# First layer's weighted sums: adding up in PSUM instead of in SBUF

## The reference, cut to what matters

```python
ex = jnp.exp(scores - seg_max[dst])
denom = jax.ops.segment_sum(ex, dst, num_segments=N)
w = ex / denom[dst]
agg = jax.ops.segment_sum(w[:, :, None] * V[src], dst, num_segments=N)
deg = jax.ops.segment_sum(jnp.ones((src.shape[0],), jnp.float32), dst, num_segments=N)
msgs = jnp.where(deg[:, None, None] > 0, agg, V)
```

## Time and profile before

| what | us |
|---|---|
| median of 3 timed runs | 5717.69 (5707.19 to 5718.29) |
| profiled execution: its span, first to last instruction (the page gives no other time of it) | 5709.5 |
| TensorE busy, of the span | 4142.4 (73%) |
| VectorE busy | 2438.6 (43%) |
| GpSimd busy | 2168.6 (38%) |
| ScalarE busy | 1163.7 (20%) |
| `attend_phase`, first instruction to the next phase's first | 900.0 to 1266.8 |

### The profile page before, as it was taken

How to read it: one execution, slowest core, us unless ns; L and a number is a source line. 1 busy time by engine, 2 the same in 40 slices (tenths; PEclk the granted TensorE clock), 3 DMA queues, 4 the chain that set the end, 5 groups by cost and what they waited for, 6 DMA issues and landing times. The chain is left out here.

```text
span 5709.5 us, 67954 instructions
## 1 busy us (share of the span) xinstructions
PE 4142.4 (73%) x19769; PEld 3142.0 (55%) x19769; DVE 2438.6 (43%) x4746; ACT 1163.7 (20%) x2671; POOL 2168.6 (38%) x2090
## 2 busy tenths in 40 slices
PE   5788884654816666799976999455559999555668
PEld 2555553443614444599975888333437677334445
DVE  4577778877234444356655000421223222212244
ACT  1233330001220000232322444100004333000023
POOL 0566654554436666000000210466650000566621
PEclk9888887996958888899986999677779999777789
DMA  2677874530743223210012998233330000233310
GB/s 77 208 243 241 250 215 151 162 98 23 235 128 88 85 86 86 86 38 8 7 41 82 336 323 281 89 88 93 87 97 26 1 1 16 75 91 88 91 37 23
DMA packets 375879, 639.34 MB, mean 112 GB/s; under 512 B 73053, under 2 KB 270072, under 8 KB 375424
## 3 DMA queue, kind: packets, MB, share of 16 engines
q1 hardware_dynamic: 275262, 342.97, 18.4%
q0 software_dynamic: 100288, 292.14, 17.6%
HBM read 526.37 MB, written 108.57 MB: 111 GB/s over the span
## 5 line engine op out<-in xcount | busy, mean ns | idle before, releaser
L2554 PE MATMUL sum_ps<-gathered_rows,hit 128*125 (+1 forms) x3328 | 1061.5, 477 | 842.0 <-issue 561.2
L2468 POOL DMA_INDIRECT gathered_rows<-k_table,index x1176 | 1160.8, 987 | 1281.1 <-ACT index L2457 717.6
L2554 PEld LDWEIGHTS sum_ps<-gathered_rows,hit 128*125 128x125 f32 (+1 forms) x3328 | 744.9, 235 | 1158.0 <-issue 1033.1
L97 POOL DMA_INDIRECT rows_all<-kv_table,src_of_visit x416 | 448.5, 1078 | 310.6 <-issue 135.5
L2538 DVE TENSOR_TENSOR node_sums<-node_sums,sum_ps 125x256 f32 x244 | 102.3, 419 | 918.0 <-DMA composed<-in_L_gnn_b 495.7
L2457 ACT ACTIVATE index<-src_of_chunk 128x4 int32<-128x4 int32 x294 | 59.2, 205 | 1647.0 <-DMA gathered_rows<-k_table,index 1581.1
L777 PE MATMUL ps_q<-q,hit_t 125*128 x832 | 322.5, 473 | 5.9 <-issue 5.2
L1057 PE MATMUL ps_sum<-summand,hit 128*125 128x261 f32 x832 | 211.6, 397 | 147.1 <-DVE odd_sums L1017 123.2
L2538 DVE TENSOR_TENSOR window_sums<-window_sums,sum_ps 126x256 f32 x344 | 144.8, 421 | 348.2 <-PE sum_ps L2554 183.0
L2762 PE MATMUL qk_ps<-window_sums,composed 128*128 128x126 f32 (+1 forms) x2400 | 292.1, 279 | 0.0
L1996 DVE TENSOR_TENSOR y<-out_ps,b 128x256 f32<-128x256 f32 x120 | 50.9, 424 | 551.2 <-PE out_ps L1895 464.0
(11 more groups left out here) (478 smaller groups left out, 6714.6 us busy)
## 6 DMA issues: line engine op xcount, KB each, us to landing
w<-in_L_ffn_W SPq DMA_DIRECT2D x112, 1024.0 KB
v_kept<-rows_all SPq DMA_DIRECT2D x104, 512.0 KB
v_rows<-v_kept SPq DMA_DIRECT2D x104, 512.0 KB, 3.6
gathered_rows<-k_table,index POOLq DMA_INDIRECT x1176
w<-in_L_ffn_w SPq DMA_DIRECT2D x64, 256.0 KB
b<-in_L_ffn_b SPq DMA_DIRECT2D x88, 128.0 KB
y_slots<-y SPq DMA_DIRECT2D x32, 256.0 KB
y_slots<-y SPq DMA_DIRECT2D x56, 128.0 KB
```

The source lines that it names most:

```text
L97: pool.indirect_dma_start(env.ring[:, k % KEPT_RING, i, :], None, env.kv_table, bass.IndirectOffsetOnAxis(env.src_of_visit[:, k * VB + i:k ...
L2468: pool.indirect_dma_start(self.rows[:, (q % SLOTS) * CHUNKS + c, :], None, self.table, bass.IndirectOffsetOnAxis(self.index[:, q % SLOTS, ...
L2554: mm = pe.matmul(sum_ps[0:rows, k % banks, 0:D], hit[:, g % (lead + 1), i * chunks + c, :], gather.rows[:, ds(first[i] + c, 1), :].rearran ...
```

## The change

Eight PSUM banks (`SUM_BANKS`) replace the two batches of four. A visit's bank is its tile number modulo 8, and every matmul adds onto what the bank holds (`start=False`). VectorE clears all banks once at the start of the phase and no longer adds; it makes the hits and, in ScalarE's place, copies the weights into `summand`. TensorE loads, per batch, the four bank numbers in one call and the last visit's tile number plus one (`turn_of_visit`) in another, and waits until so many banks have been cleared. ScalarE goes through the 25 tiles: it loads the number of the tile's last visit (`end_of_tile`), waits until so many visits have been multiplied, copies the bank to `sums`, and writes zeros over the bank. `odd_sums` and its final add are gone. `setup_phase` computes the three new tables in five VectorE instructions and one transpose on TensorE.

```diff
+                    if out is None:
+                        done(v.tensor_copy(bank_i[:], tile_bc[j][0:1, :]))
+                        done(v.tensor_scalar(env.bank_of_visit[:], bank_i[:], SUM_BANKS - 1, None, ALU.bitwise_and))
+                        done(v.tensor_scalar(env.turn_of_visit[:], tile_bc[j][0:1, :], 1.0, None, ALU.add))
+                        done(v.memset(env.end_of_tile[:], VT))
+                        done(v.tensor_copy(env.end_of_tile[:, 0:T - 1], bank[1][0:1, 441:440 + T]))
...
+                    if j == 0:
+                        pe.transpose(bank[1][0:1, 440:440 + T], key[0:T, 0:1], env.ident[0:T, 0:T])
...
-        odd_sums = sb(env, st, "odd_sums", [P, T, VC])
-        sum_of = [env.sums, odd_sums]
-        ps_sum = ps(env, st, "ps_sum", [128, 2, VB, 512])
+        ps_sum = ps(env, st, "ps_sum", [128, SUM_BANKS, 512])
...
             def _(v):
-                def add(k, tiles):
...
-                        v.tensor_tensor(here, here, ps_sum[0:P, k % 2, i, 0:VC], ALU.add).then_inc(summed, 1)
...
-                v.memset(env.sums[:], 0.0).then_inc(cleared, 1)
-                v.memset(odd_sums[:], 0.0).then_inc(cleared, 1)
...
-                v.tensor_tensor(env.sums[:], env.sums[:], odd_sums[:], ALU.add)
+                v.memset(ps_sum[:], 0.0).then_inc(filled, 1)
+                v.wait_ge(filled, 2)
+                for k in range(batches):
+                    if k >= SLOTS:
+                        v.wait_ge(multiplied, (k - SLOTS + 1) * VB)
                     make_hits(v, env, hit[:, k % SLOTS], env.rel_dst, 128, k).then_inc(hits_made, 1)
+                    v.tensor_copy(summand[:, k % SLOTS, :, D:D + HEADS], env.scores[:, k * VB:(k + 1) * VB, :]).then_inc(copied, 1)
             def _(act):
+                act.wait_ge(filled, 2)
+                act.sem_inc(cleared, SUM_BANKS)
+                for t in range(T):
+                    here = ps_sum[0:P, t % SUM_BANKS, 0:VC]
+                    upto = act.value_load(env.end_of_tile[0:1, t:t + 1], min_val=1, max_val=VT)
+                    act.wait_ge(multiplied, upto)
+                    act.activation(env.sums[:, t, :], here, ACT.Copy).then_inc(kept, 1)
+                    if t + SUM_BANKS < T:
+                        act.wait_ge(kept, t + 1)
+                        act.activation(here, env.ones[0:P, 0:1].to_broadcast([P, VC]), ACT.Copy, scale=0.0).then_inc(cleared, 1)
             def _(pe):
+                pe.wait_ge(filled, 2)
                 for k in range(batches):
                     slot = k % SLOTS
+                    _, banks = nc.values_load_multi_w_load_instructions(env.bank_of_visit[0:1, k * VB:(k + 1) * VB],
+                                                                        engines=[mybir.EngineType.PE], min_val=0, max_val=SUM_BANKS - 1)
+                    turn = pe.value_load(env.turn_of_visit[0:1, k * VB + VB - 1:(k + 1) * VB], min_val=1, max_val=T)
+                    pe.wait_ge(cleared, turn)
                     pe.wait_ge(hits_made, k + 1)
+                    pe.wait_ge(copied, k + 1)
                     pe.wait_ge(weighed, k + 1)
-                    if k >= 2:
-                        pe.wait_ge(summed, (k - 1) * VB)
                     for i in range(VB):
-                        mm = pe.matmul(ps_sum[0:P, k % 2, i, 0:VC], hit[:, slot, i, 0:P], summand[:, slot, i, :],
-                                       start=True, stop=True)
-                    mm.then_inc(multiplied, 1)
+                        pe.matmul(ps_sum[0:P, ds(banks[i], 1), 0:VC].rearrange("p o n -> p (o n)"), hit[:, slot, i, 0:P],
+                                  summand[:, slot, i, :], start=False, stop=True, skip_group_check=True).then_inc(multiplied, 1)
```

More of the change, by code:

```diff
@@ L200, in setup_phase @@
         key = sb(env, st, "key", [128, 4])
+        bank_i = sb(env, st, "bank_i", [1, VT_PAD], I32)
         cmp = [sb(env, st, f"cmp{j}", [128, -(-c // 128), v]) for j, (_, _, c, v, _) in enumerate(passes)]
@@ L807, in _ @@
                 batch_loop(act, batches, SLOTS, one_batch)
+SUM_BANKS = 8
 RUNS = 32
@@ L969, in attend_phase @@
         summand = sb(env, st, "summand", [128, SLOTS, VB, VC])
-        odd_sums = sb(env, st, "odd_sums", [P, T, VC])
-        sum_of = [env.sums, odd_sums]
-        ps_sum = ps(env, st, "ps_sum", [128, 2, VB, 512])
-        cleared, hits_made, multiplied, summed, weighed, copied = [ph.sem() for _ in range(6)]
+        ps_sum = ps(env, st, "ps_sum", [128, SUM_BANKS, 512])
+        filled, hits_made, multiplied, weighed, copied, cleared, kept = [ph.sem() for _ in range(7)]
         own_landed = ph.sem()
@@ L992, in _ @@
             def _(pool):
-                pool.memset(summand[:], 1.0).then_inc(cleared, 1)
-                pool.wait_ge(cleared, 3)
+                pool.memset(summand[:], 1.0).then_inc(filled, 1)
+                pool.wait_ge(filled, 2)
                 for k in range(batches):
@@ L998, in _ @@
                     if k >= SLOTS:
-                        pool.wait_ge(multiplied, k - SLOTS + 1)
+                        pool.wait_ge(multiplied, (k - SLOTS + 1) * VB)
                     pool.tensor_tensor(summand[:, slot, :, 0:D].rearrange("p v (h d) -> p v h d", h=HEADS),
@@ L1006, in _ @@
             def _(v):
-                def tile_of(k, i):
-                    return v.value_load(env.tile_of_visit[0:1, k * VB + i:k * VB + i + 1], min_val=0, max_val=T - 1)
-                def add(k, tiles):
[L1012 to L1016, removed]
-                        v.tensor_tensor(here, here, ps_sum[0:P, k % 2, i, 0:VC], ALU.add).then_inc(summed, 1)
-                        if k + 1 < batches:
-                            following.append(tile_of(k + 1, i))
-                    return following
@@ L1022, in hits @@
-                def hits(k):
-                    make_hits(v, env, hit[:, k % SLOTS], env.rel_dst, 128, k).then_inc(hits_made, 1)
-                v.memset(env.sums[:], 0.0).then_inc(cleared, 1)
-                v.memset(odd_sums[:], 0.0).then_inc(cleared, 1)
[L1027 to L1035, removed]
@@ L1036, in _ @@
-                v.wait_ge(summed, batches * VB)
-                v.tensor_tensor(env.sums[:], env.sums[:], odd_sums[:], ALU.add)
+                v.memset(ps_sum[:], 0.0).then_inc(filled, 1)
[3 more added lines that the diff above has]
+                        v.wait_ge(multiplied, (k - SLOTS + 1) * VB)
+                    make_hits(v, env, hit[:, k % SLOTS], env.rel_dst, 128, k).then_inc(hits_made, 1)
+                    v.tensor_copy(summand[:, k % SLOTS, :, D:D + HEADS], env.scores[:, k * VB:(k + 1) * VB, :]).then_inc(copied, 1)
@@ L1051, in _ @@
                     pe.wait_ge(hits_made, k + 1)
+                    pe.wait_ge(copied, k + 1)
                     pe.wait_ge(weighed, k + 1)
-                    pe.wait_ge(copied, k + 1)
-                    if k >= 2:
-                        pe.wait_ge(summed, (k - 1) * VB)
                     for i in range(VB):
-                        mm = pe.matmul(ps_sum[0:P, k % 2, i, 0:VC], hit[:, slot, i, 0:P], summand[:, slot, i, :],
-                                       start=True, stop=True)
@@ L3339, in build @@
         env.tile_of_visit = sb(env, x_stack, "tile_of_visit", [1, VT_PAD], I32)
+        env.bank_of_visit = sb(env, x_stack, "bank_of_visit", [1, VT_PAD], I32)
+        env.turn_of_visit = sb(env, x_stack, "turn_of_visit", [1, VT_PAD], I32)
+        env.end_of_tile = sb(env, x_stack, "end_of_tile", [1, T], I32)
         env.src_of_visit = sb(env, x_stack, "src_of_visit", [128, VT_PAD], I32)
```

## The result

The changed kernel takes 5659.26 us (median of 4 runs, 5657.38 to 5668.87); the kernel before, on the same chip, 5717.99 us (4 runs, 5707.19 to 5721.81). The ratio is 0.9909, with a 95% interval of 0.9893 to 0.9924: faster by 0.9%, and 3 us from the forecast of 5662. The profiled execution took 5658.99 us with a span of 5657.1, against a span of 5709.5 before. Of the four executions of four_loads, further down, one took 11185.87 us; its ratio leaves that one out, its median does not.

The account below looks back on a forecast made before the run. VectorE's hits and adds bound the kernel before; TensorE's instruction queue would bound it next. Loop -39.7, head -8.5, tail -9.0 and setup +1.7 gave -55.5 us, from the median 5717.7 to 5662 us; range 5600 to 5700.

Parts of the forecast that it names:

- the loop: The 104 batches of the changed phase: time per batch p falls from 3.285 to 2.9 us, -39.7 us.
- the head: Phase start to first passes: one shorter memset, first passes at 907.8 instead of 916.33 us, -8.5 us.
- the tail: Last pass to next phase: only the last copy, 1.1 us instead of 10.1, -9.0 us.
- setup: Setup phase: five added VectorE instructions, which TensorE waits for, lie on the path, +1.7 us (0 to 2.5).
- ScalarE's banks: Loop: waiting for ScalarE to copy and zero a bank costs nothing; 17 us in all if ScalarE were not ahead.
- GpSimd: Loop: GpSimd's products take 1.9 us each, with about 1 us idle, waiting for TensorE.
- The pair's rule: Loop: GpSimd and VectorE take turns, so p is at least 2.3 us, 2.5 if the scores copy waits too.
- Rival 1: Loop: checks cost little, GpSimd and VectorE bound it; p 2.4, 5611 us, up to 5640; chance 0.20.
- Rival 2: Loop: the call becomes four loads, TensorE's queue is slower than VectorE was; p 3.9, 5765 us; chance 0.11.
- Rival 3: Loop: register loads are slower than 0.3 us; p 3.2 to 3.3, 5693 to 5703 us; chance 0.07.

Follow-up runs that it names:

- four_loads: The changed kernel with four loads of one bank number each in place of one load of four: ratio 1.0111 to the kernel before.
- three_bank_checks: The changed kernel with one of the four bank-number range checks left out: batch time 2.700 us at the mean, 2.647 at the median.
- no_bank_checks: The changed kernel with the four bank numbers loaded without range checks, the tile number's check kept: median batch time 2.385 us.
- hits_from_psum: no_checks_reduce with the hit reading iota from PSUM and four sum banks instead of eight: batch time 1.859 us at the median, 2.108 at the mean.
- no_checks_reduce: The changed kernel with bank numbers unchecked and VectorE's copy of scores made by a reduction: median batch time 2.307 us.

## Why the prediction was right

The mechanism of the loop, the head and the tail held; the loop was off by 6.9 us and setup, whose step failed, by 2.1 the other way. The four terms of the sum came to -51.6 us instead of -55.5. That the median lies only 3 us from the forecast is in part luck: the gain by the spans is 52.4 us, by the medians 58.7, and the score phase alone scatters by 21.

- **The loop.** Forecast p 2.9 and -39.7 us, measured 2.967 and -32.8. TensorE's queue is what the forecast named, with one load and four checks as it was read from the way the call is written. The term is mis-sized by 0.067 us a batch, 6.9 us in all, and most of that is rounding: the forecast's own parts, 2.0 for a group of two loads, 0.84 for three checks and 0.10 for one more wait, add up to 2.94, the median measured is 2.951, and it took 2.9. A check costs 0.28 as forecast (0.27 to 0.30 by three_bank_checks); a load of four registers is 0.04 longer than one of one. The mean lies 0.016 above the median, 1.6 us in the loop: the first batch took 3.63 us, and some others 3.05 to 3.11, whose cause stays open.
- **ScalarE's banks,** costed at nothing, cost nothing that the trace shows: the four waits that bear its name are gaps of the usual 0.9 to 1.0 us.
- **GpSimd.** The prediction looked for products of 1.9 us with about 1 us idle. They took 2.35 with 0.6 idle, since each still meets a hit. With the queue as the bound this did not touch the time.
- **The head.** Forecast -8.5, measured -9.0. First passes were forecast 7.8 us behind the phase's start and came at 7.3. The memset of PSUM took 3.47 us for 4096 columns; 3.45 was worked out from the SBUF memset of the earlier trace rows. The estimate of 4.26 us, worked out from the 1.04 ns that the Trainium skill (PSUM — Partial Sum Buffer, "Specifications (TRN2)") gives for a 2-byte element, is not what this memset of 4-byte elements shows; the measurement decides.
- **The tail.** Forecast -9.0, measured -9.4: the copy of 0.39 us, and 0.3 us from its end to the next phase.
- **Setup.** The step that failed: +1.7 us was forecast "on the path", -0.4 measured. The five instructions cost what was said and did delay TensorE, but what they delay is not what ends the phase. Setup in after, then in before:

```profile
28.47 0.43 SPq L231 DMA_DIRECT2D x<-in_x  x1
...
51.67 0.50 PEld L374 LDWEIGHTS bank<-sel,rows_f 98*128 98x128 f32 x2 [4.42 <-DVE sel L310]
...
66.12 4.98 SPq L233 DMA_DIRECT2D quad_key_kept<-quad_key  x1
...
78.06 1.08 DVE L1265 BATCH_NORM_STATS2 moments_nodes<-x 125x6 f32<-125x256 f32 x3 [2.36 <-DVEq L501]
```

```profile
28.25 0.43 SPq L230 DMA_DIRECT2D x<-in_x  x1
...
64.01 7.44 SPq L232 DMA_DIRECT2D quad_key_kept<-quad_key  x1
...
78.40 0.75 DVE L1272 BATCH_NORM_STATS2 moments_nodes<-x 125x6 f32<-125x256 f32 x2 [4.83 <-DVEq L492]
```

The weight load of `sel` came 1.8 us later (51.67, 49.88 in the earlier trace rows). VectorE had 4.83 us to spare before the next phase and has 2.36 left. SyncE waits there for two transfers, the load of `x`, issued long before the five instructions (28.25 and 28.47 us), and the store of `quad_key`, which stands behind it in the same queue. The trace's packets show which is late. The last of the 3125 rows of `x` (1,024 bytes each) landed at 76.70 us before and 76.36 after, the last eight of the store's 128 packets came behind them, until 77.34 and 76.99, and the next phase began 0.93 to 0.94 us later. That distance, and the 1.57 to 1.58 us from the last row of `x`, are the same in all eleven profiled executions. So the end of `x` sets the phase's end, and the store, issued 2.1 us later, still finds itself waiting behind it. In the ten executions with the five instructions the next phase began at 77.6 to 79.4 us, in the one without at 78.3: the -0.4 is scatter, and the cost is hidden. That the forecast asked only whether TensorE waits, and not what the barrier waits for, was the mistake.
- **The pair's rule.** The Trainium skill (SBUF — State Buffer, "Who interferes with whom") says that a VectorE instruction of the kinds named in the prediction and a GpSimd instruction that reads SBUF exclude each other. The trace agrees: the copy takes 1.87 us beside a product and 0.16 without one, and with one hit input in PSUM hit and product fall to 0.69 and 1.91 us; whether the copy runs in a two-port mode no run shows. The pair did not set the time of after; with the copy in it its floor is 2.385 us, as no_bank_checks shows, below the 2.5 that the prediction drew from the rule.
- **The rivals.** Rival 1 (p 2.4) did not come, since the checks are paid; its bound shows in the kernel without bank checks, 2.468 at the mean. Rival 2 is four_loads. Rival 3, slow loads, did not come: after's loads keep 0.30 to 0.35 us.

## What to carry to other kernels

A loop whose instructions take register values can be bound by an engine's instruction queue, which no busy share shows: add up loads, checks and waits of one turn, and compare the sum with the turn. Ask for neighbouring words in one load, and leave the range check out where the making of the value already bounds it (here the low three bits of a tile number): that gave 0.57 us a batch, the shorter copy nothing. And before a cost is put on the path, look for what the next barrier waits for.

## What the runs showed of the hardware

- A copy of 16 columns took 1.87 us on VectorE beside GpSimd's products, 0.16 to 0.17 with none running (no_bank_checks), and 0.16 as a reduce beside them. The records show no wait: the time is inside the instruction.
- One load fills four registers in 0.34 us, one register takes 0.30; the check of a loaded value takes 0.28 us of the queue.
- With iota in PSUM the hit fell from 2.14 to 0.69 us and GpSimd's product from 2.29 to 1.91 (hits_from_psum against no_checks_reduce).
- The view of waits put 86.5 us on a hit that belonged to a later batch. With the copy made short, the name changed and the time did not.
- The last eight packets of a store of 128 landed behind the rows of `x` that were ahead of it in the queue, 4.6 us after the other 120.
